# Splitting the next layer's projection weights and building its rotary tables one layer ahead, in second sets, with the tables on GpSimd

## Reference

```python
def attn_layer(x, Wqkv, qs, ksc, Wo):
    qkv = x @ Wqkv                       # Wqkv: 128 x 3072 of this layer
    q, k, v = jnp.split(qkv, 3, -1)      # 16 heads of 64
    q = l2norm(q) * qs                   # qs, ksc: 64 scales of this layer
    k = l2norm(k) * ksc
    q = q * cos * scale + rotate_half(q) * sin * scale
    k = k * cos / scale + rotate_half(k) * sin / scale
    out = local_attention(q, k, v)       # causal, window of 32, softmax
    return out @ Wo

def ffn_layer(x, g, bln, W1, b1, W2, b2):
    hg = layernorm(x) * g + bln
    a, gate = jnp.split(hg @ W1 + b1, 2, -1)   # W1: 128 x 682
    return a * gelu(gate) @ W2 + b2
...
x = attn_layer(x, ...) + x
x = ffn_layer(x, ...) + x
```

## Time and profile before

| | |
|---|---|
| median of 3 runs | 4092.55 us (4092.03 to 4094.78) |
| profiled execution | 4086.93 us, span 4085.1 us |
| mean granted TensorE clock | 0.981 |
| HBM traffic | 45.33 MB read, 35.52 MB written |
| idle of VectorE before adding Wo's result (L1413) | 228.6 us, waiting for TensorE |
| idle of GpSimd before rot<-rot,rn (L1450) | 292.4 us, waiting for ScalarE's rn |

### The profile page before, as it was taken

One profiled execution on the slowest core, in us unless ns is written; L12 is line 12 of the kernel. 1 busy time (PEld: TensorE's weight loads), 2 busy tenths in 40 slices (PEclk: granted clock), 3 DMA queues, 4 the chain that ended last, 5 costly groups with the idle time before them and its releaser, 6 DMA issues. The chain is left out here.

```text
span 4085.1 us, 101499 instructions
## 1 busy us (share of the span) xinstructions
PE 3804.2 (93%) x30384; PEld 3094.1 (76%) x30384; DVE 3499.8 (86%) x11903; ACT 3250.3 (80%) x11174; POOL 3061.3 (75%) x3387
## 2 busy tenths in 40 slices
PE   7888887799999999999999999999999999999997
PEld 5777776578777778777778877878777777777875
DVE  5677776699999999999999999999999999999995
ACT  1555555589898889888989888989888988888985
POOL 2333333588888888888888888888888888888883
PEclk9999999799999999999999999999999999999998
DMA  4222222000000000000000000000000000000000
GB/s 152 79 83 83 83 83 72 22 5 2 2 2 2 28 2 2 2 2 26 4 2 2 2 7 23 2 2 2 2 28 2 2 2 2 7 3 2 2 2 22
DMA packets 76219, 86.71 MB, mean 21 GB/s; under 512 B 13622, under 2 KB 69396, under 8 KB 74836
## 3 DMA queue, kind: packets, MB, share of 16 engines
q1 hardware_dynamic: 75732, 80.87, 6.1%
HBM read 45.33 MB, written 35.52 MB: 20 GB/s over the span
## 5 line engine op out<-in xcount | busy, mean ns | idle before, releaser
L1272 ACT ACTIVATE p<-p,mx 128x128 f32<-128x128 f32 x3072 | 1192.8, 401 | 3.5 <-DVE mx L1357 2.8
L1450 POOL TENSOR_TENSOR rot<-rot,rn 128x512 f32<-128x512 f32 x768 | 805.0, 1048 | 293.3 <-ACT rn L1287 292.4
L1461 POOL TENSOR_TENSOR rot<-own_crossed 128x512 f32<-128x512 f32 x768 | 989.1, 1288 | 0.1
L1446 POOL TENSOR_TENSOR p<-p,ri 128x512 f32<-128x512 f32 x768 | 802.9, 1046 | 24.1 <-DVE ri L1396 24.1
L1357 DVE CUSTOM_DVE_ANT_0 p<-bank_pair,band_f 128x128 f32<-128x128 f32 x3072 | 704.7, 285 | 30.4 <-issue 22.2
L1272 ACT ACTIVATION_READ_ACCUMULATOR p<-p,mx 128x1 f32 x3072 | 612.7, 199 | 0.0
L454 PE MATMUL bank<-wqkv_hi,xs_lo 128*128 128x512 f32 x1152 | 556.6, 483 | 50.9 <-DVE own_crossed L1390 47.6
L1305 ACT ACTIVATE sq<-bank 128x512 f32<-128x512 f32 x768 | 452.6, 589 | 160.0 <-PE bank L456 159.3
L1371 DVE TENSOR_REDUCE ss<-sq 128x8 f32<-128x512 f32 x768 | 521.9, 680 | 9.1 <-ACT sq L1305 9.1
L1408 DVE COPY pTl<-bank 128x512 f32<-128x512 f32 x768 | 511.7, 666 | 16.9 <-PE bank L1176 8.0
L1385 DVE TENSOR_TENSOR own_crossed<-bank,rot_tab 128x512 f32<-128x512 f32 x768 | 522.4, 680 | 0.2
(11 more groups left out here) (198 smaller groups left out, 7353.4 us busy)
## 6 DMA issues: line engine op xcount, KB each, us to landing
pos_scratch<-pos_sb SPq DMA_DIRECT2D x32, 1020.0 KB, 4.4
sc<-pos_scratch SPq DMA_DIRECT2D x32, 512.0 KB, 4.0
wqkv_raw<-in_L_ffn_Wqkv SPq DMA_DIRECT2D x6, 1536.0 KB, 6.8
ctx_sb<-in_ctx SPq DMA_DIRECT2D x32, 128.0 KB, 3.5
wo<-in_L_ffn_Wo SPq DMA_DIRECT2D x6, 512.0 KB, 4.0
mrow<-in_mask_BxS_fk SPq DMA_DIRECT2D x1, 2048.0 KB, 7.7
x_all<-in_x SPq DMA_DIRECT2D x4, 512.0 KB, 8.7
out<-res SPq DMA_DIRECT2D x8, 256.0 KB, 2.3
```

What stands on the lines that cost most here:

```text
L1272: last = nc.scalar.activation(p[:, j, h, :], p[:, j, h, :], ACT.Exp, bias=mx[:, j, h:h + 1], scale=-1.0, accum_out=psums[:, j, h:h + 1])
L1446: nc.gpsimd.tensor_tensor(p[:, j, :, :], p[:, j, :, :], ri[:, j, :].unsqueeze(2).to_broadcast([128, G, T]), ALU.mult).then_inc(L["pn"], 1)
L1450: nc.gpsimd.tensor_tensor(rot[:, (k - 8) % 4, :, :], rot[:, (k - 8) % 4, :, :], rn[:, (k - 8) // 2 % 4, (k - 8) % 2, :].unsqueeze(2).to_br ...
L1461: nc.gpsimd.tensor_tensor(rot[:, (k - 7) % 4, :, :], own[:, (k - 7) % 4, :, :], crossed[:, (k - 7) % 4, :, :], ALU.add).then_inc(L["rot0"], 1)
```

## The change

- There are two sets of the q and k weights (`wqk`, by the parity of the layer) and still one of v (`wv`). To pay for the room, the raw weights have two buffers of one group each, v's ring goes from 16 to 12 units, and the output's tiles `zq` and `res` lie in the rotary buffers.
- A layer's groups 0 to 3 are split in the layer before: ScalarE at step 12, GpSimd at step 14, of quads 2 to 5. The v groups stay where they were.
- The tables have two sets. GpSimd builds those of layer l + 1 at step 14 of quad 6 of layer l, and those of layer 0 at step 4 of its quad 0. VectorE only waits for the semaphore.
- W1 is rounded by ScalarE at step 13 of quad 1, and GpSimd subtracts in two halves, at step 15 of quad 1 and step 0 of quad 2.
- SyncE loads the weights in six pieces of 256 KB, each behind a wait for the split that frees its buffer; in part 1 four of them stand ahead of the ctx loads of iterations 1 and 2. Its loop over the layers is written out.

```diff
-        wqkv_raw = sb("wqkv_raw", [128, 3, INNER])
+        wqkv_raw = sb("wqkv_raw", [128, 2, 2 * G * DL])
...
+        def load_weight_group(sp, l, e):
...
+            if l + e > 1:
+                wait_apart(sp, L["wqkv_split"], l * WEIGHT_GROUPS + e - 1)
+            sp.dma_start(dst, src).then_inc(L_raw[e % 2], 16)
...
                     if reused(first, k, 0, 2):
                         wait_apart(sp, S1["ctxT_mm"], u0 - 1)
+                    if isinstance(first, int) and 0 < u0 < WEIGHT_GROUPS // 2:
+                        for e in (2 * u0, 2 * u0 + 1):
+                            load_weight_group(sp, 0, e)
...
-        v_sb = sb("v_sb", [128, 16, G, DL])
+        VALUES = 12
+        v_sb = sb("v_sb", [128, VALUES, G, DL])
...
+            def ahead(self, k):
+                if self.k != k or self.l == LAYERS - 1 or not 2 <= self.q < 2 + UB:
+                    return None
+                return self.q - 2
...
             def next_layer(l):
-                wait_apart(sp, L["wqkv_split"], l * WEIGHT_GROUPS)
-                load_wqkv(l)
                 wait_apart(sp, L["tab"], l)
                 load_scales(l)
...
                 wait_apart(sp, Fm["y_mm"], l * QUADS)
                 load_w2(l)
+                if l + 1 < LAYERS:
+                    wait_apart(sp, L["proj_qk"], l * UNITS)
+                    for e in range(WEIGHT_GROUPS):
+                        load_weight_group(sp, l + 1, e)
...
# ScalarE
-                if at.renew() and k < UB:
-                    if k == 0:
-                        act.wait_ge(L["wqkv_in"], 16 * (l + 1))
-                    round_group(k)
+                e = at.ahead(12)
+                if e is not None:
+                    round_group(l + 1, e)
+                if at.layer_start(1) and k == 13:
+                    act.wait_ge(Fm["w1_in"], 16 * (l + 1))
+                    if l > 0:
+                        act.wait_ge(Fm["a"], 3 * QUADS * l)
+                    nc.scalar.activation(w1_hi[:, :], w1_raw[:, :], ACT.Copy).then_inc(Fm["w1_hi"], 1)
...
# VectorE
                 if at.layer_start(0) and k == 5:
-                    if l > 0:
-                        wait_apart(dve, L["own_crossed"], l * UNITS)
-                    dve.wait_ge(L["scl_in"], 32 * (l + 1))
-                    nc.vector.tensor_tensor(rot_tab[:, :, :], rot_base[:, 0:2, :], qk_scl[:, :, :], ALU.mult)
-                    nc.vector.tensor_tensor(rot_x[:, :, :].rearrange("p (a h) n -> p a h n", a=2), rot_base[:, 2:4, :].unsqueeze(2).to_broadcast([128, 2, G, DL]),
-                                            qk_scl[:, :, :].unsqueeze(2).to_broadcast([128, 2, G, DL]), ALU.mult).then_inc(L["tab"], 1)
                     dve.wait_ge(L["tab"], l + 1)
...
# GpSimd
+                def rotary_tables(l):
+                    if l > 1:
+                        wait_apart(pool, L["own_crossed"], (l - 1) * UNITS)
+                    wait_apart(pool, L["scl_in"], 32 * (l + 1))
+                    nc.gpsimd.tensor_tensor(rot_tab[:, l % 2, :, :], rot_base[:, 0:2, :], qk_scl[:, :, :], ALU.mult)
+                    nc.gpsimd.tensor_tensor(rot_x[:, l % 2, :, :].rearrange("p (a h) n -> p a h n", a=2), rot_base[:, 2:4, :].unsqueeze(2).to_broadcast([128, 2, G, DL]),
+                                            qk_scl[:, :, :].unsqueeze(2).to_broadcast([128, 2, G, DL]), ALU.mult).then_inc(L["tab"], 1)
...
-                if at.renew() and 0 < k <= UB:
-                    keep_rest(k - 1)
+                e = at.ahead(14)
+                if e is not None:
+                    keep_rest(l + 1, e)
+                if l == 0 and at.layer_start(0) and k == 4:
+                    pool.wait_ge(rot_in, 16)
+                    rotary_tables(0)
+                if l < LAYERS - 1 and at.layer_start(2 + UB) and k == 14:
+                    rotary_tables(l + 1)
```

More of the change, by code:

```diff
@@ L424, in build @@
         HALF = H0 // 2
+        def load_weight_group(sp, l, e):
+            w = Wqkv[bass.ds(l, 1)].rearrange("a p n -> (a p) n")
+            if e < UB:
+                src = w.rearrange("p (c n) -> p c n", c=3)[:, 0:2, e * G * DL:(e + 1) * G * DL]
+                dst = wqkv_raw[:, e % 2, :].rearrange("p (c n) -> p c n", c=2)
+            else:
+                src = w[:, 2 * INNER + (e - UB) * 2 * G * DL:2 * INNER + (e - UB + 1) * 2 * G * DL]
+                dst = wqkv_raw[:, e % 2, :]
+            if l + e > 1:
+                wait_apart(sp, L["wqkv_split"], l * WEIGHT_GROUPS + e - 1)
+            sp.dma_start(dst, src).then_inc(L_raw[e % 2], 16)
         def part1_sync(sp):
@@ L929, in swapped, with weight_group @@
             return t.rearrange("p h (s n) -> p h s n", s=2)[:, :, ::-1, :]
-        def weight_group(e):
-            cols = (slice(0, 2), slice(e * G * DL, (e + 1) * G * DL)) if e < UB else (slice(2, 3), slice((e - UB) * 2 * G * DL, (e - UB + 1) * 2 * G * DL))
-            return [w[:, cols[0], cols[1]] for w in (wqkv_hi, wqkv_lo, wqkv_raw)]
+        def weight_group(l, e):
+            raw = wqkv_raw[:, e % 2, :]
+            if e < UB:
+                hi, lo = [w[:, l % 2, :, e * G * DL:(e + 1) * G * DL] for w in wqk]
+                return hi, lo, raw.rearrange("p (a n) -> p a n", a=2)
+            hi, lo = [w[:, (e - UB) * 2 * G * DL:(e - UB + 1) * 2 * G * DL] for w in wv]
+            return hi, lo, raw
         WEIGHT_GROUPS = UB + UB // 2
@@ L1008, in layer_start, with table @@
                 return isinstance(self.q, int) and self.q == q
+            def ahead(self, k):
+                if self.k != k or self.l == LAYERS - 1 or not 2 <= self.q < 2 + UB:
+                    return None
+                return self.q - 2
+            def table(self, d):
+                return (self.l - 1 if self.q == 0 and self.k < d else self.l) % 2
             def renew(self):
@@ L1040, in first_attention @@
             def first_attention():
-                load_wqkv(0)
+                for e in range(2):
+                    load_weight_group(sp, 0, e)
                 load_scales(0)
@@ L1131, in emit @@
                             c = 2 * w + h // 2
-                            last = nc.tensor.matmul(oT_ps[rows, c * T:(c + 1) * T], v_sb[:, u % 16, h, :], pTl[:, u % 4, h, :], start=True, stop=True)
+                            last = nc.tensor.matmul(oT_ps[rows, c * T:(c + 1) * T], v_sb[:, u % VALUES, h, :], pTl[:, u % 4, h, :], start=True, stop=True)
                     last.then_inc(L["PV"], 1)
@@ L1163, in emit @@
                     g = (k - 9) % UB
-                    split_product(v_ps[:, :], [x[:, (k - 9) // UB % 4, :] for x in xs], [w[:, 2, g * G * DL:(g + 2) * G * DL] for w in wqkv]).then_inc(L["proj"], 1)
+                    split_product(v_ps[:, :], [x[:, (k - 9) // UB % 4, :] for x in xs], [w[:, g * G * DL:(g + 2) * G * DL] for w in wv]).then_inc(L["proj"], 1)
                 if at.ffn(12):
@@ L1471, in emit @@
                     nc.gpsimd.tensor_tensor(xs_lo[:, j, :], shifted(at.own_batch(2), 1).rearrange("p a n -> p (a n)"), xs_hi[:, j, :].bitcast(F32), ALU.subtract).then_inc(L["xs"], 1)
-                if at.renew() and 0 < k <= UB:
-                    keep_rest(k - 1)
-                if at.renew() and k in (6, 8):
-                    keep_rest(UB + (k - 6) // 2)
-                if at.layer_start(1) and k == 14:
-                    wait_apart(pool, Fm["w1_in"], 16 * (l + 1))
-                    if l > 0:
-                        wait_apart(pool, Fm["u"], 3 * QUADS * l)
-                    nc.gpsimd.tensor_copy(w1_hi[:, :], w1_raw[:, :]).then_inc(Fm["w1_hi"], 1)
-                if at.layer_start(1) and k == 15:
-                    pool.wait_ge(Fm["w1_hi"], l + 1)
-                    nc.gpsimd.tensor_tensor(w1_lo[:, :], w1_raw[:, :], w1_hi[:, :].bitcast(F32), ALU.subtract).then_inc(Fm["w1_split"], 1)
+                e = at.ahead(14)
[6 more added lines that the diff above has]
+                    rotary_tables(l + 1)
+                if at.renew() and k in (6, 8):
+                    keep_rest(l, UB + (k - 6) // 2)
+                if at.layer_start(1) and k == 15 or at.layer_start(2) and k == 0:
+                    wait_apart(pool, Fm["w1_hi"], l + 1)
+                    cols = slice(0, FF) if k == 15 else slice(FF, 2 * FF)
+                    last = nc.gpsimd.tensor_tensor(w1_lo[:, cols], w1_raw[:, cols], w1_hi[:, cols].bitcast(F32), ALU.subtract)
+                    if k == 0:
+                        last.then_inc(Fm["w1_split"], 1)
             stream(pool, emit)
@@ L1518, in _ @@
             first_ffn()
-            with sp.Fori(1, LAYERS) as l:
+            for l in range(1, LAYERS):
                 next_layer(l)
```

52 lines of the change are left out of this document (26 added, 26 removed).

## The result

The changed kernel takes 4024.8 us in the median (4024.23 to 4029.2, 4 runs), the one before beside it 4092.29 (4085.27 to 4094.78). The ratio is 0.984, with a 95% interval of 0.9823 to 0.9857. I had forecast 4060 us, a gain of 32 us.

What follows compares the result with a forecast made beforehand. TensorE and VectorE nearly full, plus a VectorE wait at layer starts. 4086.9 - 53.4 - 0.7 + 3.2 + 16 + 1.5 + 1.5 = 4055.0; with 5.6 on top 4060.6, stated as 4060 us, range 4037 to 4080.

Steps and rivals of the forecast that it cites:

- The stall: At five layer starts VectorE's table instructions wait for GpSimd; removal gives back 10.68 us each, 53.4 us.
- The page of the Trainium skill: Its shared-port rule would make the tables' removal worth some 3 us a boundary, 15 in all; the forecast followed the rows.
- Added work on GpSimd: Splits and tables at step 14, v splits in quad 0: 0.74 us cover each, 3.2 us a layer, 16 us added.
- v splits: Two splits staying at steps 6 and 8 of quad 0, without the stall as cover: 0.3 us a layer.
- Rival (a): GpSimd's pauses take all of its added work, so the 16 us go: 4044 us, chance 0.18.
- the bias copies: VectorE's two copies of b1, step 15 of quad 1: 0.8 us longer two times in six, 1.5 us added.
- catch-up: The quad after each stall runs quicker, 66.22 us against 66.87; without the stall this goes, 3.2 us lost.
- From the profile to the median: The runs' median, 4092.55 us, lies 5.6 above the profiled execution, so 5.6 was added to the sum.
- Taken as 0: ScalarE's roundings, V's ring, the weight loads and the program's end were each counted as 0 us.
- (b): Most added time lies on the path, as TensorE has no slack: 29 us more, 4090, chance 0.09.
- (c): In quad 1 the bias copies wait as the table did, until GpSimd runs dry: 45 us, 4105, chance 0.05.
- (d): Tables come late on GpSimd and VectorE waits at the old place: about 4085 us or more, chance 0.02.

Runs made afterwards that it cites:

- before_tables_pool: The kernel before, with the tables alone moved to GpSimd, in two sets built a layer ahead: 4045.74 us, ratio 0.9901 to the kernel before.
- tables_dve: The kernel after, with each layer's tables built by VectorE again at the old place: 4028.08 us, ratio 0.9855 to the kernel before.
- w1_pool: The kernel after, with W1's rounding and whole subtraction back on GpSimd at steps 14 and 15 of quad 1: 4036.91 us, ratio 0.9871 to the kernel before.

## Why the prediction was right and wrong

- **The stall.** Right: 53.4 us forecast, 53.25 measured, nothing left at the boundary, clock 1.00. The words "this is no work but a wait inside the instruction" hold. The forecast tied the wait to GpSimd but not to the bunch; before_tables_pool and tables_dve show that either part alone takes it away. Where it counts seven of GpSimd's instructions in the wait, the trace has nine ends, eight before the last.
- **The page of the Trainium skill.** "SBUF — State Buffer", section "SBUF: two separate sides", has the second comer blocked until the other's instruction is over. In tables_dve the trace agrees (1.52 us, one GpSimd instruction). In the kernel before it agrees for `rot_tab` (1.20) and does not for `rot_x` (9.25), right behind it. Going by the row for this kernel was right.
- **Added work on GpSimd: the step that failed.** It read "Behind step 14 GpSimd has step 15's normalisation of the rotated vectors, which TensorE's transposes wait for. It ends at 2134.33 (2133.28 + 1.05) and the transposes start at 2135.20: 0.87 apart". Those transposes are step 14's. Step 15's start at 2139.78, 5.45 us after their vectors, and the real room, pauses and distance together, is 3.1 us, so the +16 us for splits, tables and v splits had no ground: for splits and tables it was 0. That is 14.5 of the 35.8 us of the miss (4060.6 by the sum, 4024.8 measured). Rival (a), "the pauses take all of the added GpSimd work", is what happened; its 4044 was missed by the bias copies.
- **Quad 0.** The terms +3.2 (catch-up) and 0.3 a layer (v splits) make 4.7; 6.8 was measured: the catch-up was worth 2.7, and the v groups cost 0.8 a layer with no stall to cover them.
- **The bias copies: the second step.** "I take that two times in six: 1.5 us", with a bound of -9 if all are short. They were all short, and it was worth -11 in the profile and -12 by w1_pool. With the forecast's +1.5 this is 12.6 us of the miss. The forecast looked at the half split behind the copies. Of W1's work ahead of them it said that it "lay in a pause and is taken as 0, and could give back under 1 us a layer". In the kernel before nothing is left of such a pause: GpSimd has run 17.6 us without one when the copies come. With that work lessened, a pause of 1.3 us stands ahead of them, and w1_pool shows that it gave back 2.4 us a layer (12.1 in five).
- **From the profile to the median: the rest.** The forecast added 5.6 us (4092.55 - 4086.93). The kernel after lay 4.4 under its profiled execution. That is the 10 us left of the miss (the larger loss in quad 0 took 2.1 us off it). It is spread between runs, which no term of the forecast stood for.
- **Taken as 0:** the ScalarE roundings, the rings, the loads in pieces and the end. The steady quads, at 66.85 us, allow no cost for them there. TensorE takes iteration 1's ctx at 70.14, 0.26 later than before (near 71 was forecast). The start's +1.9 in the profile is no measured loss: kernels with the same part 1 have their first product anywhere from 752.1 to 757.4 us.
- **Rivals (b), (c), (d).** No quad with a split grew, no copy waited longer than 0.95 us, and no engine waited for the tables.

Open: what decides whether VectorE's instruction gets in at the end of GpSimd's running one (0.7 to 1.5 us) or only when GpSimd is dry (2.8 to 9.25). The long waits all meet a GpSimd that is behind, but so do `rot_tab` in the kernel before and nine short first copies. For the copies 0.03 us of arrival goes with the outcome, for the tables it does not.

## What to carry to other kernels

Before charging work added to an engine, pair its products with their readers unit by unit, and add up the pauses ahead of each: the nearest later start of the reader may belong to the step before. Look for tiny SBUF-to-SBUF instructions of VectorE beside a packed GpSimd: their durations in the profile (ns min/median/max) show the wait, and it reached the critical path here (in the kernel before, 2.97 us of copies made quad 1 2.6 to 4.2 us longer than a steady one, 1.88 us made it 1.5 longer). When a stall needs two causes, taking away either removes it, so test the parts singly before paying for both, and look at what each leaves behind: here 46 us of 46.5 for one and 37 for the other.
